# Recurrence stage: smaller input-offset and maxima instructions on VectorE, and the inter-chunk factor in four matmuls over a repeated column

## The reference, cut to what matters

```
x = x + recurrence(layernorm(x), ctx, ctx, ...)
log_f    = log_sigmoid(fg);  cs = cumsum(log_f)
log_D    = where(tril, cs_t - cs_s, -inf) + ig_s
m        = max(log_D, axis=-1)
D        = exp(log_D - m)
C        = (q k^T / sqrt(64)) * D
h        = (C / (max(|sum C|, exp(-m)) + 1e-6)) v
```

## Time and profile before

| | us |
|---|---|
| median of 3 runs | 1745.97 |
| lowest, highest | 1745.84, 1746.75 |
| the profiled execution, its own time | 1738.19 |
| its span in the trace | 1736.4 |
| mean granted clock of TensorE over the span | 0.979 |

### The profile page before, as it was taken

How to read it: one execution, slowest core, us unless ns; L and a number is a source line. 1 busy time by engine, 2 the same in 40 slices (tenths; PEclk the granted TensorE clock), 3 DMA queues, 4 the chain that set the end, 5 groups by cost and what they waited for, 6 DMA issues and landing times. The chain is left out here.

```text
span 1736.4 us, 58211 instructions
## 1 busy us (share of the span) xinstructions
PE 1554.1 (90%) x21967; PEld 1257.7 (72%) x22095; DVE 1398.5 (81%) x2826; ACT 1154.4 (66%) x2775; POOL 1262.1 (73%) x1235
## 2 busy tenths in 40 slices
PE   4899999999999999999999999679999969998983
PEld 3777777777777777777777777579999945555541
DVE  2588888888888888888888888768766458999998
ACT  3677777777777777777777776422334338888873
POOL 1477787777778777777877877757887527979764
PEclk9899999999999999999999999889999989999998
DMA  6133322233222333222323211173565354777787
GB/s 219 46 99 100 99 94 93 93 103 102 94 93 93 99 100 100 94 93 93 103 97 98 93 51 39 45 294 112 169 205 147 98 121 112 213 231 218 224 228 208
DMA packets 82020, 217.72 MB, mean 125 GB/s; under 512 B 13136, under 2 KB 14544, under 8 KB 72784
## 3 DMA queue, kind: packets, MB, share of 16 engines
q1 hardware_dynamic: 71504, 180.42, 33.4%
q0 software_dynamic: 10240, 33.56, 6.7%
HBM read 146.82 MB, written 67.11 MB: 123 GB/s over the span
## 5 line engine op out<-in xcount | busy, mean ns | idle before, releaser
L315 POOL TENSOR_TENSOR rec_hn<-rec_hn,rec_out_w 128x512 f32<-128x512 f32 x128 | 183.3, 1432 | 124.5 <-DVE rec_hn L747 124.5
L293 POOL TENSOR_TENSOR rec_hrs<-rec_harg,rec_minus_half 128x8 f32<-128x8 f32 x128 | 253.9, 1983 | 10.0
L767 DVE TENSOR_TENSOR rec_x_ring<-rec_x_ring,rec_hn 128x512 f32<-128x512 f32 x128 | 88.7, 693 | 121.8 <-POOL rec_hn L315 121.4
L543 ACT ACTIVATE rec_d<-rec_l_ps 128x512 f32<-128x512 f32 x256 | 151.4, 592 | 52.2 <-PE rec_l_ps L447 50.8
L713 DVE TENSOR_TENSOR rec_c<-rec_s_ps,rec_d 128x512 f32<-128x512 f32 x256 | 166.4, 686 | 13.8 <-ACT rec_d L543 4.9
L1013 PE MATMUL exp_q_ps<-exp_wqkv,exp_rows_t 128*128 128x192 f32 x1024 | 177.1, 327 | 0.0
L1344 POOL TENSOR_TENSOR out_x_half<-out_x_half,ln_b 128x512 f32<-128x512 f32 x104 | 132.7, 1282 | 54.3 <-DVE out_z L1520 53.5
L964 POOL DMA_INDIRECT exp_x_rows<-x_scratch,rowid x128 | 135.0, 1055 | 45.8 <-issue 24.2
L467 PE MATMUL rec_o_ps<-rec_v_one,rec_c 128*64 128x65 f32 x4096 | 151.9, 226 | 16.8 <-DVE rec_c L713 16.8
L1013 PEld LDWEIGHTS exp_q_ps<-exp_wqkv,exp_rows_t 128*128 128x128 f32 x1024 | 165.4, 191 | 0.1
L1073 ACT ACTIVATE exp_rows_t<-exp_t_ps 128x512 f32<-128x512 f32 x128 | 69.4, 594 | 139.5 <-PE exp_t_ps L1001 139.5
(11 more groups left out here) (217 smaller groups left out, 4417.2 us busy)
## 6 DMA issues: line engine op xcount, KB each, us to landing
rec_x_ring<-in_x SPq DMA_DIRECT2D x128, 256.0 KB, 2.9
rec_ctx_ring<-in_ctx SPq DMA_DIRECT2D x128, 256.0 KB, 3.0
x_scratch<-rec_x_ring SPq DMA_DIRECT2D x128, 256.0 KB, 2.0
out_x_half<-x_scratch SPq DMA_DIRECT2D x104, 256.0 KB, 5.0
out<-out_x_half SPq DMA_DIRECT2D x104, 256.0 KB, 5.6
exp_wqkv<-in_wqkv SPq DMA_DIRECT2D x4, 1536.0 KB, 8.9
v_all<-x_scratch SPq DMA_DIRECT2D x24, 256.0 KB, 5.0
out<-v_all SPq DMA_DIRECT2D x24, 256.0 KB, 5.4
```

Source lines behind the costliest of these rows:

```text
L293: nc.gpsimd.tensor_tensor(hrs[:, G % 2], harg[:, G % 2], mhalf[:], ALU.pow).then_inc(hrs_done, 1)
L315: nc.gpsimd.tensor_tensor(h, h, w8[:], ALU.mult).then_inc(hw_done, 1)
L543: nc.scalar.activation(dst[:].rearrange("p k s -> p (k s)"), l_ps[:], ACT.Exp).then_inc(l_read, 1)
```

## The change

Three places of the recurrence stage are written otherwise:

- `input_offsets`: two tensor_scalar instructions of one element per partition each. Mean is the one tensor input, the reciprocal deviation is a per-partition scalar read from SBUF, and -1 is an immediate.
- `g_rows`: `mend` is made by four tensor_scalar instructions, one for each chunk end, each of 8 partitions and 8 elements. The identity is the tensor input, the maximum at the chunk's end a per-partition scalar.
- `rows` and `log_inter`: DVE writes a second copy, from PSUM to partitions 64 to 127 of `rows`: for chunks 1 to 3 the last column of the previous chunk, repeated 128 times (384 columns of bf16). `sel_q` holds the selectors in its upper 64 partitions and the negated ones in its lower 64, so that one matmul does what two did. `log_inter` issues four matmuls in place of eight.

```diff
-                nc.tensor.matmul(o, sel_q[:, 0, k, :], src[:, c * P:(c + 1) * P], start=(k == 0), stop=False)
-                mm = nc.tensor.matmul(o, sel_q[:, 1, k, :], src[:, c * P - 1:c * P].broadcast_to([P, P]),
-                                      start=False, stop=(k == KC - 1))
+                mm = nc.tensor.matmul(o, sel_q[:, k, :], src[:, c * P:(c + 1) * P], start=(k == 0), stop=(k == KC - 1))
...
-            vec.tensor_copy(sel_q[:, 0, :, o], m4[:, e, :, o])
-            vec.tensor_scalar(sel_q[:, 1, :, o], m4[:, e, :, o], -1.0, None, ALU.mult)
+            vec.tensor_copy(sel_q[0:64, :, o], m4[0:64, e, :, o])
+            vec.tensor_scalar(sel_q[64:P, :, o], m4[0:64, e, :, o], -1.0, None, ALU.mult)
...
-            vec.scalar_tensor_tensor(xrn[:, i:i + 2, 1], xagg[:, i:i + 2, 0], -1.0, xrn[:, i:i + 2, 0], ALU.mult, ALU.mult
-                                     ).then_inc(x_rs, 1)
+            vec.tensor_scalar(xrn[:, i, 1:2], xagg[:, i, 0:1], xrn[:, i, 0:1], -1.0, ALU.mult, ALU.mult)
+            vec.tensor_scalar(xrn[:, i + 1, 1:2], xagg[:, i + 1, 0:1], xrn[:, i + 1, 0:1], -1.0, ALU.mult, ALU.mult
+                              ).then_inc(x_rs, 1)
...
-                vec.tensor_tensor(mend[:], mrow[:, P - 1::P].unsqueeze(2).broadcast_to([NH, NC, NH]),
-                                  ident[0:NH, 0:NH].unsqueeze(1).broadcast_to([NH, NC, NH]), ALU.mult).then_inc(mend_done, 1)
+                for c in range(NC):
+                    end = vec.tensor_scalar(mend[:, c, :], ident[0:NH, 0:NH], mrow[:, (c + 1) * P - 1:(c + 1) * P], None,
+                                            ALU.mult)
+                end.then_inc(mend_done, 1)
...
-                vec.tensor_copy(rows[p][0:64, :], sm_ps[0:64, 0:256].bitcast(BF16)).then_inc(sm_read, 1)
+                read = sm_ps[0:64, 0:256].bitcast(BF16)
+                vec.tensor_copy(rows[p][0:64, :], read)
+                vec.tensor_copy(rows[p][64:P, P:].rearrange("p (c s) -> p c s", c=NC - 1),
+                                read[:, P - 1:S - 1:P].unsqueeze(2).broadcast_to([64, NC - 1, P])).then_inc(sm_read, 1)
```

More of the change, by code:

```diff
@@ L120, in recurrence_stage @@
     sel_m = sb("sel_m", [P, 2, KC, P], BF16)
-    sel_q = sb("sel_q", [P, 2, KC, P], BF16)
+    sel_q = sb("sel_q", [P, KC, P], BF16)
     gw_in = sb("gate_w_in", [P, 3, KC, NG])
```

## The result

| | us |
|---|---|
| changed kernel, median of 4 runs | 1766.55 (1764.65 to 1768.18) |
| kernel before, 4 runs beside it | 1746.36 (1745.84 to 1748.31) |
| ratio, 95% interval | 1.0113 (1.0096 to 1.0131) |
| the profiled execution after, its own time, span | 1765.52, 1763.7 |

The account below looks back on a forecast made before the run. DVE was taken to bound part A, PE part B: +0.39 - 0.22 = +0.17 us, times 29 = +4.9; -1 for other sequences, +1 for order: 1746 to 1751. Own range 1747 to 1759, with rivals 1726 to 1773.

Parts of the forecast that it names:

- The two parts and who bounds them: Each recurrence sequence splits in two: DVE sets the length of part A, PE that of part B.
- part A: Stretch of a sequence from the scores of step 1 to the products of step 2; claimed to be DVE's length.
- part B: Stretch of a sequence from the products of step 2 to the next step 1; claimed to be PE's length.
- Four matmuls, -0.22 in part B: `log_inter`: each call 0.22 us shorter; only the third, in part B, counts, as DVE can start its weigh earlier.
- The second copy, no cost: DVE's second copy of the rows takes 0.5 us in DVE's slack; done 0.4 us before PE asks, costing nothing.
- `mend`, +0.39 in part A: First of four instructions waits for POOL's centred values as before; three more add 0.13 us each on DVE.
- rival 2: tensor_scalar does not wait for POOL, so `mend` saves 0.48 us in part A; -20 us, 1726; chance 0.22.
- The offsets, nothing: Two offset instructions in steps 1 and 3 are covered by waits for POOL or do not wait; 0 us.
- Rival 1: Offsets wait twice for POOL in step 3, PE stands some 0.65 us for the rows; +24 us, 1770; chance 0.25.
- PE's wait for `rec_c`, 0.57 to 1.4: Sign in the trace: PE's wait before step 2's products grows from 0.57 to about 1.4 us in the mean.
- The allowance of +1 us for the order of DVE and POOL: An earlier weigh lets DVE come ahead of POOL in some sequences, moving part A by up to 0.1 us; +1 us.
- PE's busy time, 20 us less: Sign in the changed trace: PE's busy time falls by some 20 us while DVE's rises.

Follow-up runs that it names:

- e1_matmuls: Kernel before with only the four matmuls for eight and the second copy of the rows; 1754.4 us, ratio 1.0055.
- e2_mend4: Kernel before with only `mend` made by four tensor_scalar instructions; 1761.2 us, ratio 1.0089.
- e7_mend4_psum: Changed kernel with its four `mend` instructions reading the identity from PSUM instead of SBUF; 1736.6 us, ratio 0.9941.
- e3_offsets: Kernel before with only the two offset instructions of one element each; 1745.0 us, ratio 0.9994.
- e8_offs2: Changed kernel with offset instructions of two elements in place of one, the second result unused; 1782.4 us, ratio 1.0214.
- e12_psum_keys: Kernel before with `mend` as one instruction reading the identity from PSUM, and POOL's weighted keys ahead of the `log_f` sum in step 1; 1721.5 us, ratio 0.9854.
- e11_mats_psum_keys: e12_psum_keys with the four matmuls and the second copy of the rows added; 1709.7 us, ratio 0.9793 against the kernel before.
- e9_step0_eight: e1_matmuls with each of chunk 1's four matmuls issued twice, same result; 1750.6 us, ratio 1.0027 against the kernel before.

## Why the prediction was right in direction and wrong in size

The range of 1726 to 1773 holds the measured 1766.6 only because it took in both rivals. Of the 20 us the forecast had one cause right, `mend`; the order at the port it had priced too low, and the half clock it did not have. The direction follows from `mend` alone; that the time lies in the range is no merit of the sum.

- *The two parts and who bounds them.* Right. Every kernel above moves by what its part A loses on DVE or its part B on PE.
- *Four matmuls, -0.22 in part B.* Right: -0.23 in e1_matmuls, -0.18 in the changed kernel. DVE's readiness was seen rightly too: the weigh starts at 711.47, 0.13 us after its copy.
- *The second copy, no cost.* Right: 0.55 us (0.5 taken), and among PE's waits from 100 to 1100 us there is none for `rec_rows` in the changed kernel, and a single one, of 1.0 us, in e1_matmuls (of 0.7 in before).
- *`mend`, +0.39 in part A.* Right: +0.38 in e2_mend4, with the first of the four 1.05 us long and done 0.02 us after POOL's centred values, and the others 0.21 long and 0.13 apart. By that rival 2 falls, and by e7_mend4_psum the wait is priced. One reading was wrong: that PE would find `mend` done. In the changed kernel it waits for it in nearly all sequences (L398 above), behind which it would have stood anyway.
- *The offsets, nothing.* Right: e3_offsets. Rival 1 had price and mechanism right and its condition wrong (e8_offs2).
- *PE's wait for `rec_c`, 0.57 to 1.4.* In kind. It grew, but to 1.14 only (1.19 in the 26 sequences). The prediction let all of PE's 0.44 us reach this wait. None did in the changed kernel: 0.20 went into the wait for ACT's `rec_x_t` and 0.25 into that for `mend`, so that the stand grew by what part A grew. In e1_matmuls, where `mend` is early, only the first of the two is there, and about 0.2 of the 0.44 arrived.
- *The allowance of +1 us for the order of DVE and POOL.* Here the step failed. The prediction named the mechanism ("an earlier weigh lets DVE come ahead of POOL") and priced it at up to 0.1 us in some sequences. It is 0.25 us in the mean, 7 us in all, with POOL's sum held in 24 of 29 sequences of e1_matmuls: the start of the sum and of the head norm stood 0.24 us apart, and the same 0.22 us that part B gained eats just that. The distance stood in rows that I had not set side by side, the sum and the head norm of step 1. So the net of the four matmuls is nothing instead of -0.22: all their gain in part B comes back in part A.
- *The clock.* Not in the sum at all. Five sequences at 1.1 us are 5 to 6 us. In the earlier trace rows PE stands 0.59 us and is granted the full clock throughout; that with a stand twice as long the clock falls in one sequence of six, nothing in the trace of before shows.
- *PE's busy time, 20 us less.* Only 8.4 in the recurrence, in part because matmuls at half clock take longer; 21.0 from e12_psum_keys to e11_mats_psum_keys, which have no such stretch there.

With the sizes measured, the prediction's own sum is (0.38 + 0.25 - 0.2) x 29 = 12.5, and 5.5 for the clock: 18, where the recurrence has 18.3 and the medians 20. The other 2 us lie in the stages behind it and within what their times vary from run to run.

What is shown and what is argued: that the order at the port costs part A 0.25 to 0.3 us is shown by e9_step0_eight, where the old order comes back and part A with it; the three kernels with the keys first show that POOL's place in step 1 sets the residual (4.79 us after the weigh) and that up to 0.9 us of part A hangs on it. That the half clock follows from the length of PE's stand is a pattern over thirteen kernels and no more: none with a mean stand of up to 0.62 us has a stretch in the 26 sequences counted, all five with 0.90 or more have three to six. Within the changed kernel the stand does not tell the sequences apart: it is 1.19 us in the five that have such a stretch and 1.19 to 1.20 in nearly all the others. What picks the five is open. No kernel lengthened the stand and did nothing else.

## What to carry to other kernels

Where two engines share a port, look in the profile for pairs of instructions that start within a few tenths of a microsecond of each other: a gain that moves one of them can turn the order round, and the price is set by what the loser holds up, not by its own size. An instruction queued behind one that waits for another engine is the first candidate to be moved ahead. A small operation that waits for the port is better given an input from PSUM than split: the split multiplied the instructions and kept the wait.

## What the runs showed of the hardware that was not expected

- A POOL instruction of 32 elements takes 0.25 us when it starts 0.02 us or more ahead of a DVE instruction with two inputs from SBUF, and 0.74 to 0.81 us when it starts between 0.01 us ahead of it and 0.05 us behind it, in all kernels here; the mean over a kernel in which the order is turned is 658 to 721 ns.
- One element per partition keeps a tensor_scalar from SBUF clear of POOL (0.20 us with POOL's keys, 731.19 to 732.23, running), two do not (1.09 us).
- POOL's powers of two and of four elements do not hold DVE's head norm, which has two inputs from SBUF: it starts 0.28 to 0.45 us after that of two elements (0.70 us long) in 29 sequences of the kernel before and takes its usual 0.69 us. For the long power of eight elements, 2.0 us, no long DVE instruction with two SBUF inputs starts inside it, so it stays open.
- The granted clock fell from full to 0.50 in the middle of a recurrence in which PE is busy some nine tenths of the time (30.07 of 33 us in the window before), starting in PE's stand of 1.19 us, and came back within the same sequence; the price was 1.1 to 1.5 us each in the mean. In the experiments such a stretch started 0.1 to 1.0 us after that stand's end, in or just behind the products.
